# Attention and expert kernel on one core: the loads and weight splits of the first batch, the place of the second expert's split, and the order of row loads, stores and output sums are changed

## The chip, the cores and the metric

The kernel runs on one core of one Trainium2 chip. The metric is the device time of the whole kernel in microseconds (us), the median of three runs. "PE" is TensorE, "DVE" VectorE, "ACT" ScalarE, "POOL" GpSimd, and "SP" the engine that here only issues transfers.

## The reference

Two residual blocks over 16 batches of 128 tokens with 512 features, all in float32:

```python
x = x + tanh(g_xattn) * xattn(layernorm(x), ctx, pos, pos, Wq, Wkv, Wout, bout)
x = x + tanh(g_ffn) * ffn(layernorm(x), gate_w, w1, w2, shared_w1, shared_w2)
# xattn: 32 heads of 16, rotary embedding by position on q and k, softmax over 128 context rows
# ffn:   softmax router over 16 experts, top 6 of them per token; expert: silu(x w1a) * (x w1b) @ w2,
#        width 352; a shared expert of width 704 for every token
```

## The kernel before

Every float32 product is made of three fp32r matmuls. Both factors are split into a "hi" part (a copy rounded to fp32r) and a "lo" part (the value minus hi), and hi·hi, hi·lo and lo·hi are summed in PSUM. So each activation and each weight has a copy (hi) and a subtraction (lo) before PE can use it.

**Phase A** (`phase_a`) is attention, normalisation and routing. It is a software pipeline of rounds. A round works on five batches at once, one for each stage LOAD, PROJECT, ATTEND, TAIL and PLACE, and is cut into eight units `u`. The order of the work in a round is written out by hand for each engine (`one_round`). The first six and the last four rounds are peeled, and what happens once only hangs on them:

- `sync` issues the loads. At the start it issues x of batch 0, Wq, the constants, positions, gates, bout and gate_w, which all count into one semaphore, `small_in`; then the first context, Wkv, Wout and x of batch 1. POOL's first `rsqrt`, PE, ACT and DVE all wait for `small_in`.
- `first_work` on ACT and DVE splits Wq ("q", 128x2048), Wkv ("kv") and Wout ("o"): ACT writes hi, DVE lo. DVE also works out the rotary angles (`first_angles`, seven small instructions), of which ACT takes the sine.
- POOL makes the rotary pairs (`pairs`, two instructions for q and two for k), the inverse deviations (`rsqrt`), and scatters each batch's rows to the experts' lists in DRAM (`scatter`, six indirect transfers). It also splits the experts' weights: `split_w1` (8 copies and 8 subtractions of 128x352) and `split_w2`. The splits of the first expert (place 0) stand in rounds 1 to 3 (`early_weights`), the w1 split of the second one (place 1) in the last round with an ATTEND stage.

**Phase B** (`phase_b`) runs tiles of 128 rows: 6 early tiles of the shared expert, 111 routed blocks, then the rest of the shared expert. Step i of PE is `down(i-2)`, `transpose_act(i-1)`, `up(i)`. Beside it DVE turns the rows of tile i+1 (`turn_x`) and makes `x_low`, `a_low` and `gated` (the activation, whose PE transposition opens the next step); ACT makes `x_high`, `a_high`, `gate` (silu) and copies y out of PSUM (`y_out_of_psum`). SP loads the rows of tile i+3 (`load`: a table value, four transfers for `xr`, one for `xw`), stores y of tile i-2 (`store`), and for the early tiles loads x1 of batch i (`load_x1_early`), to which DVE's `add_early` adds the early tile's result. `add_early` waits for x1 and for the store that last read its y buffer. In the last part `combine_rows` and `combine` sum the six gathered expert rows of each token, and `finish` adds the shared expert's sum in PSUM (`y_banks`) and so sets the bank free.

An order on each engine is fixed when the program is written: an instruction that waits holds up all that stand behind it on its engine.

## Time and profile before

| | |
|---|---|
| Median of three runs | 1397.35 us (1395.98 to 1401.92) |
| Profiled execution, its own time | 1397.16 us |
| Its span, first to last instruction | 1395.0 us |
| PE busy | 1321.3 us, 95% |
| DVE, POOL, ACT busy | 774.5, 697.9, 570.1 us |
| Phase A | about 0 to 480 us |
| Phase B | about 480 us to the end |

The 2.2 us between the span and the profiled execution's own time lie before the first and after the last instruction. The profile shows, per instruction, the start, the duration, and in brackets how long the engine had been idle and what it waited for.

### The profile page before, as it was taken

Reading aid. Unit: us, or ns where it says so; the run is one execution under the profiler, and the core shown is the slowest. Engines: PE = TensorE matmul, PEld = TensorE weight load, DVE = VectorE, ACT = ScalarE, POOL = GpSimd, SP = SyncE. Lnnn points to the kernel's source line nnn. Section 1 sums busy time; section 2 is a strip of 40 time slices with the busy share of each in tenths; the row PEclk is TensorE's granted clock in tenths of the full one; section 3 lists DMA queues with packets and bytes.
Section 4 is the critical chain, followed back from the end, with each engine's and each line's share of the span. In section 5 each row is a group of like instructions: output and inputs, shape, how many; then the busy total and the mean of one; then the engine's idle time right before and its main releaser. Section 6 shows DMA issues by size and latency. Waiting matters only on the chain.

```text
span 1395.0 us, 32586 instructions
## 1 busy us (share of the span) xinstructions
PE 1321.3 (95%) x8414; PEld 1133.8 (81%) x8415; DVE 774.5 (56%) x1572; ACT 570.1 (41%) x1374; POOL 697.9 (50%) x968
## 2 busy tenths in 40 slices
PE   3799999999996898999999999999999999999998
PEld 2566766766764788999999999999999999998887
DVE  4467777777767763444444444444444444356776
ACT  3667667667664422332323333232333323221121
POOL 4354554544545654297442445555542350285673
PEclk9899999999997999999999999999999999999999
DMA  5032332322323665544354444444434443266885
GB/s 202 17 110 83 128 115 80 137 104 80 144 80 108 216 210 182 183 144 133 102 149 146 146 148 144 151 144 141 128 112 148 145 151 85 87 191 206 263 247 157
DMA packets 152398, 196.97 MB, mean 141 GB/s; under 512 B 33155, under 2 KB 103300, under 8 KB 149524
## 3 DMA queue, kind: packets, MB, share of 16 engines
q1 hardware_dynamic: 130292, 104.03, 24.8%
q0 software_dynamic: 22048, 92.23, 19.6%
q8 instruction: 29, 0.48, 0.2%
q14 instruction: 29, 0.24, 0.1%
HBM read 122.11 MB, written 74.07 MB: 141 GB/s over the span
## 4 chain that ended last, share of the span: by engine, by line
PE 75%; DVE 8%; ACT 6%; issue 5%; SPq 2%; DMA 1%; ACTq 0%; DVEq 0%; POOL 0%; POOLq 0%
PE bank L1562 35%; PE bank L1607 19%; PE bank L713 5%; ACT soft L599 4%; PE bank L738 4%; PE bank L1574 3%; PE bank L720 2%; PE bank L752 2%; PE bank L825 2%; DVE smax L1013 2%; PE bank L769 1%; DVE x L1058 1%; DVE attn L1052 1%; DVE stats L1061 1%; SPq L1346 1%
## 5 line engine op out<-in xcount | busy, mean ns | idle before, releaser
L1562 PE MATMUL bank<-w_hi,x_hi 128*128 (+1 forms) x1144 | 289.9, 334 | 0.0
L1562 PE MATMUL bank<-w_hi,x_lo 128*128 (+1 forms) x1144 | 277.1, 323 | 0.0
L1562 PE MATMUL bank<-w_lo,x_hi 128*128 (+1 forms) x1144 | 277.0, 323 | 0.0
L212 POOL CAST w_hi<-w_raw 128x352 fp32r<-128x352 f32 x152 | 72.7, 526 | 369.4 <-PE bank L1562 369.4
L1502 ACT ACTIVATE silu<-bank 128x352 f32<-128x352 f32 x143 | 66.4, 464 | 410.3 <-PE bank L1562 410.3
L1678 DVE SCALAR_TENSOR_TENSOR act<-silu,row_w,bank 128x352 f32<-128x352 f32 x111 | 64.4, 580 | 290.7 <-ACT silu L1502 290.6
L1562 PEld LDWEIGHTS bank<-w_lo,x_hi 128*128 128x128 f32 x1144 | 199.2, 189 | 0.0
L1562 PEld LDWEIGHTS bank<-w_hi,x_lo 128*128 128x128 f32 x1144 | 199.0, 188 | 0.0
L1562 PEld LDWEIGHTS bank<-w_hi,x_hi 128*128 128x128 f32 x1144 | 192.6, 189 | 0.4 <-issue 0.4
L1607 PE MATMUL bank<-w_hi,a_hi 128*128 (+3 forms) x429 | 170.5, 397 | 8.9 <-ACT y L1486 3.8
L599 ACT ACTIVATE soft<-bank,smax 128x128 f32<-128x128 f32 x512 | 146.9, 380 | 76.7 <-DVE smax L1013 76.6
L1607 PE MATMUL bank<-w_lo,a_hi 128*128 (+3 forms) x429 | 170.4, 397 | 0.0
L1607 PE MATMUL bank<-w_hi,a_lo 128*128 (+3 forms) x429 | 169.7, 396 | 0.0
L1491 ACT ACTIVATE x_hi<-x_t 128x512 fp32r<-128x512 f32 x133 | 84.1, 632 | 178.3 <-DVE x_t L1652 178.3
L216 POOL TENSOR_TENSOR w_lo<-w_raw,w_hi 128x352 fp32r<-128x352 f32 x152 | 146.0, 991 | 0.0
L1657 DVE TENSOR_TENSOR x_lo<-x_t,x_hi 128x512 fp32r<-128x512 f32 x133 | 127.4, 958 | 31.1 <-ACT x_hi L1491 26.0
L1433 POOL DMA_INDIRECT gath<-y_rows,y_slots x96 | 101.5, 1057 | 48.0 <-issue 26.5
L1661 DVE TENSOR_TENSOR a_lo<-bank,a_hi 128x384 fp32r<-128x384 f32 x143 | 79.3, 554 | 72.9 <-ACT a_hi L1496 72.0
L520 POOL DMA_INDIRECT expert_rows<-row,slots x96 | 95.6, 996 | 35.5 <-issue 31.7
L1013 DVE TENSOR_REDUCE smax<-bank 128x4 f32<-128x512 f32 x128 | 85.0, 684 | 38.2 <-PE bank L738 37.2
L1607 PEld LDWEIGHTS bank<-w_hi,a_hi 128*128 128x128 f32 (+1 forms) x429 | 81.1, 189 | 22.6 <-issue 7.9
L1652 DVE STREAM_TRANSPOSE x_t<-xr 128x512 f32<-128x512 f32 x133 | 93.7, 704 | 7.9 <-DMA xr<-expert_rows 7.8
(186 smaller groups left out, 2155.4 us busy)
## 6 DMA issues: line engine op xcount, KB each, us to landing
xr<-expert_rows SPq DMA_DIRECT2D x444, 64.0 KB, 1.9
y_rows<-y SPq DMA_DIRECT2D x111, 256.0 KB, 2.1
w_raw<-in_w POOLq DMA_DIRECT2D x19, 1408.0 KB, 6.6
w_raw<-in_w POOLq DMA_DIRECT2D x19, 512.0 KB, 7.8
xr<-x_rows SPq DMA_DIRECT2D x88, 64.0 KB, 3.0
x_t<-x_rows SPq DMA_DIRECT2D x22, 256.0 KB, 4.6
x_sb<-in_x SPq DMA_DIRECT2D x16, 256.0 KB, 3.8
x_res<-in_x SPq DMA_DIRECT2D x16, 256.0 KB, 3.0
```

What stands on the lines that cost most here:

```text
L212: nc.gpsimd.tensor_copy(w1_hi[d][half][:, s], w1_raw[:, d, halves[half]]).then_inc(w_hi_made, 1)
L216: nc.gpsimd.tensor_tensor(w1_lo[d][half][:, s], w1_raw[:, d, halves[half]], w1_hi[d][half][:, s].bitcast(F32), ALU.subtract).then_inc(w1_m ...
L520: g.indirect_dma_start(rows, bass.IndirectOffsetOnAxis(slots[j][:, k:k + 1], 0), row[j][:], None)\
L599: last = a.activation(soft[u % 2][:, h, :], bank[2 + u % 2][:, h * P:(h + 1) * P], ACT.Exp, bias=smax[u % 2][:, h:h + 1])
L1013: v.tensor_reduce(smax[u % 2][:], s3, AX.X, ALU.max, negate=True).then_inc(smax_done, 1)
L1433: nc.gpsimd.indirect_dma_start(gath[b % 2][:, k, :], None, y_rows, bass.IndirectOffsetOnAxis(y_slots[:, b * 8 + k:b * 8 + k + 1], 0))\
L1491: a.activation(x_hi[j][:], x_t[:], ACT.Copy).then_inc(x_hi_done, 1)
L1562: last = nc.tensor.matmul(to[:, 0:WIDTH], xx[jt][:, d, :], w[d][half][:, cols], start=(d == 0 and xx is x_hi and w is w1_hi), stop=(d == D ...
L1607: last = nc.tensor.matmul(to[:], l[j][0:m, c, :], w[c][0:m, cols], start=(first and c == 0 and k == 0), stop=(final and c == 2 and k == 2))
L1652: v.transpose(x_t[:].rearrange("p c (i t) -> p i c t", i=4), xr[j][:].rearrange("p (i c e) -> p i c e", i=4, c=DC)).then_inc(x_turned, 1)
L1657: v.tensor_tensor(x_lo[j][:], x_t[:], x_hi[j][:].bitcast(F32), ALU.subtract).then_inc(x_lo_done, 1)
L1661: v.tensor_tensor(a_lo[j][:].rearrange("p c n -> p (c n)"), a_bank[:, 0:3 * P], a_hi[j][:].rearrange("p c n -> p (c n)").bitcast(F32), ALU ...
```

## The change

**First batch.** The constants are put in a new order, so that those needed first (identity, even/odd scales, frequencies) make a block of 141 columns with a semaphore of its own, `first_in`. The small transfers move from SP's queue to ACT's (gates: to POOL's), with their own semaphores for positions and gates. Wq is split in two parts ("q0", "q1"), Wkv in its k and v columns ("k", "v"). The angles are made before DVE's first `xn`, the "o" split one round earlier, right after the first rotary pairs. ACT runs one small Exp at the end of its first work.

**Second expert.** `split_w1(pool, 1)` is done in two halves at the end of rounds 4 and 5 instead of in one piece in the last ATTEND round.

**Phase B.** SP issues the row loads ahead of the stores, and in step 3 the load of tile 7 as well as that of tile 6. In the steps after the third ACT copies y out of PSUM ahead of `x_high` and DVE does `add_early` ahead of `turn_x`. In the last part `finish` comes ahead of `combine_rows`.

```diff
@@ gpsimd, early_weights and one_round
                 if r == 0:
-                    pool.wait_ge(w_hi_done, 1)
+                    pool.wait_ge(w_hi_done, 3)
                     load_w(nc.gpsimd, 0)
...
+                if r == 4:
+                    split_w1(pool, 1, range(0, 2))
+                if r == 5:
+                    split_w1(pool, 1, range(2, 4))
...
                 if last_round(at, ATTEND):
                     pool.wait_ge(v_mm, BATCHES)
                     clear_act()
-                    split_w1(pool, 1)
@@ scalar
-            act.wait_ge(small_in, 16 * 5)
+            a.dma_start(const[:, 0:C_FIRST], cf[:, 0:C_FIRST]).then_inc(first_in, 16)
+            a.dma_start(pos_in[:], pos).then_inc(pos_sem, 16)
+            a.dma_start(const[:, C_FIRST:C_N], cf[:, C_FIRST:C_N]).then_inc(small_in, 16)
+            a.dma_start(gate_raw[:], gate_w).then_inc(small_in, 16)
+            a.dma_start(bout_b[:], bout).then_inc(small_in, 16)
+            act.wait_ge(gates_in, 16)
             a.activation(tanh2[:], gate2[:], ACT.Tanh).then_inc(tanh_done, 1)
+            act.wait_ge(first_in, 16)
...
                 if u == 1:
                     split_weights("o")
+                    act.wait_ge(small_in, 16 * 3)
                     a.activation(gate_hi, gate_raw[:], ACT.Copy).then_inc(w_hi_done, 1)
+
+                    act.wait_ge(tanh_done, 1)
+                    a.activation(gexp[:, 0:2], tanh2[:], ACT.Exp)
@@ phase_b, sync, one_step
+                if i is None or starts_tile(i, 1):
+                    t, j, n = tile(i, at, 1)
+                    if not isinstance(t, int):
+                        load(*at(3))
+                    elif t + 2 < TILES and i != 4:
+                        load(t + 2, j, n + 1)
+                if i == 3:
+                    load(7, 1, 3)
                 if live(i, -2) and (routed(i, -2) or early(i, -2)):
                     store(*at(-2))
                     if early(i, -2) and early(i, 0):
                         load_x1_early(i)
-                if i is None or starts_tile(i, 1):
-                    t, j, n = tile(i, at, 1)
-                    if not isinstance(t, int):
-                        load(*at(3))
-                    elif t + 2 < TILES:
-                        load(t + 2, j, n + 1)
@@ phase_b, scalar and vector, one_step
                     if halves_first(i):
                         a_high(*at(-1))
+                        if routed(i, -2):
+                            y_out_of_psum(*at(-2))
                     x_high(t, j, n, before)
...
                 if halves_first(i):
                     a_low(*at(-1))
+                    if early(i, -2):
+                        add_early(*at(-2))
...
-                if early(i, -2) and i != 3:
-                    add_early(*at(-2))
                 if shared and i - 1 in sum_at and sum_at[i - 1] < BATCHES - 1:
                     combine(sum_at[i - 1])
+                if shared and i in finish_at:
+                    finish(finish_at[i])
                 if shared and i in sum_at:
                     combine_rows(sum_at[i])
-                if shared and i in finish_at:
-                    finish(finish_at[i])
```

**Order on DVE, start of the program.** The names are those of the tiles: `soft` holds the angles, `w_lo` the lo parts of Wq and Wkv. Before:

```order
L981 BN_AGGR mean<-stats 128x2 [waits stats1_done]
L986 TENSOR_SCALAR xn<-x_sb,mean,rstd 128x512 [waits rstd1_done,var1]
L924 TENSOR_TENSOR soft<-pos_in,const 128x16x4 [waits small_in]
...
L937 SCALAR_TENSOR_TENSOR soft<-soft 128x256 [waits angles]
L943 TENSOR_TENSOR w_lo<-w_raw,w_hi 128x2048 [waits w_hi_done]
L993 TENSOR_TENSOR xt_lo<-bank,xt_hi 128x512 [waits xt_hi_done,tanh_done,init_done]
L943 TENSOR_TENSOR w_lo<-w_raw,w_hi 128x2048 [waits w_hi_done]
L998 TENSOR_TENSOR c_lo<-c_raw,c_hi 128x256 [waits c_hi_done,sincos_done]
```

The same place on DVE now:

```order
L1011 BN_AGGR mean<-stats 128x2 [waits stats1_done]
L949 TENSOR_TENSOR soft<-pos_in,const 128x16x4 [waits pos_in_sem,first_in]
...
L962 SCALAR_TENSOR_TENSOR soft<-soft 128x256 [waits angles]
L1016 TENSOR_SCALAR xn<-x_sb,mean,rstd 128x512 [waits rstd1_done,var1]
L968 TENSOR_TENSOR w_lo<-w_raw,w_hi 128x1024 [waits w_hi_done]
L1023 TENSOR_TENSOR xt_lo<-bank,xt_hi 128x512 [waits xt_hi_done,tanh_done,init_done]
L968 TENSOR_TENSOR w_lo<-w_raw,w_hi 128x1024 [waits w_hi_done]
L968 TENSOR_TENSOR w_lo<-w_raw,w_hi 128x2x512 [waits w_hi_done]
```

The seven angle instructions moved ahead of `xn`, and only half of Wq's lo part now stands ahead of `xt_lo`.

**Order on SP, where phase B's own steps begin (step 3).** `x_rows<-y` is a store of an early tile, `x_t<-x_rows` the load of x1, `xr<-expert_rows` a row load, and the wait for `table_in` is the wait for the routing table. Before:

```order
L468 DMA table<-block_table 1x444 [waits table_out]
L1364 DMA x_rows<-y 128x512 [waits scattered0,scattered1,table_in,pads_out0,x2_out1,y_done,x2_out0,x1_out]
L1368 DMA x_t<-x_rows 128x512 [waits y_done]
L1341 TENSOR_LOAD table
...
L1346 DMA xr<-expert_rows 32x4x128
L1359 ISA
L1359 DMA xw<-expert_rows 128x16
L1337 TENSOR_LOAD pad_at [waits pad_zero]
```

The same place on SP now:

```order
L469 DMA table<-block_table 1x444 [waits table_out]
L1371 TENSOR_LOAD table [waits scattered0,table_in,scattered1,x2_out1,pads_out0,x2_out0,x1_out]
...
L1389 DMA xw<-expert_rows 128x16
L1371 TENSOR_LOAD table
...
L1389 DMA xw<-expert_rows 128x16
L1394 DMA x_rows<-y 128x512 [waits y_done]
L1398 DMA x_t<-x_rows 128x512 [waits y_done]
L1367 TENSOR_LOAD pad_at [waits pad_zero]
```

Two whole row loads (tiles 6 and 7) now stand ahead of the store of tile 1 and the load of x1 for batch 3.

## Rows read from the trace of the kernel before

**Rows 1.** Busy time by engine in one stretch, with granted clock (PEclk)
```profile
420.00:450.00 30.00, 18.45 (x138) 12.62 (x140) 22.61 (x39) 14.38 (x41) 18.83 (x30) 0.72 0.37 125
```

**Rows 2.** Timeline, first batch: start us, us, engine line, operation, [idle before <-releaser]
```profile
1.16 0.42 SPq L409 DMA_DIRECT2D w_raw<-in_wq  x1
...
8.79 0.19 POOL L497 TENSOR_SCALAR neg_half<-mean 128x1 f32<-128x1 f32 x1 [5.99 <-DMA gate_raw<-in_gate_w]
...
11.04 0.55 DVE L986 TENSOR_SCALAR xn<-x_sb,mean,rstd 128x512 f32<-128x512 f32 x1 [6.89 <-POOL rstd L508]
...
13.83 2.29 DVE L943 TENSOR_TENSOR w_lo<-w_raw,w_hi 128x2048 fp32r<-128x2048 f32 x1
...
16.86 0.77 PE L713 MATMUL bank<-w_hi,xt_hi 128*128 128x512 f32 x1 [4.04 <-DVE xt_lo L993]
...
30.21 0.79 PE L713 MATMUL bank<-w_hi,c_hi 128*128 128x512 f32 x1 [1.36 <-ACT k_t L659]
```

**Rows 3.** DMA issues, first 9 us: KB each, median us to landing
```profile
w_raw<-in_wq SPq DMA_DIRECT2D x1, 1024.0 KB, 5.4
```

**Rows 4.** Timeline, second and third round
```profile
35.82 1.28 ACT L599 ACT_TABLE_LOAD   x1
...
48.75 2.28 DVE L943 TENSOR_TENSOR wo_lo<-wo_raw,wo_hi 128x2048 fp32r<-128x2048 f32 x1
...
53.63 1.41 PE L738 MATMUL bank<-k_t,q_t 32*128 32x256 f32 x8 [4.03 <-ACT soft L599]
```

**Rows 5.** Timeline, POOL's half split in round 1, and the start of a full round
```profile
29.81 1.94 POOL L212 CAST w_hi<-w_raw 128x352 fp32r<-128x352 f32 x4
...
31.72 3.59 POOL L216 TENSOR_TENSOR w_lo<-w_raw,w_hi 128x352 fp32r<-128x352 f32 x4
...
122.09 0.84 POOL L488 TENSOR_TENSOR q_cos<-q_cos,q_sin 128x256 f32<-128x256 f32 x1 [1.14 <-DVE q_sin L972]
...
127.03 0.66 PE L720 MATMUL bank<-const,q_cos 128*128 128x128 f32 x4
```

**Rows 6.** Timeline, the last round with an ATTEND stage
```profile
433.31 10.26 DVE L1657 TENSOR_TENSOR x_lo<-x_t,x_hi 128x512 fp32r<-128x512 f32 x1
...
435.93 7.09 POOL L216 TENSOR_TENSOR w_lo<-w_raw,w_hi 128x352 fp32r<-128x352 f32 x8
...
444.32 1.11 PE L720 MATMUL bank<-const,attn 128*128 128x128 f32 x4 [9.75 <-DVE attn L1037]
```

**Rows 7.** Line L1657, whole run: duration ns min/median/max
```profile
L1657 DVE TENSOR_TENSOR x_lo<-x_t,x_hi x133: 677/693/10260, 433.3 to 1369.2; 128x512 fp32r<-128x512 f32 x133
```

**Rows 8.** Timeline, first steps of phase B
```profile
503.00 0.42 SPq L1368 DMA_DIRECT2D x_t<-x_rows  x1
...
506.65 0.35 SPq L1359 DMA_DIRECT2D xw<-expert_rows  x1
...
508.06 0.71 DVE L1652 STREAM_TRANSPOSE x_t<-xr 128x512 f32<-128x512 f32 x1 [1.90 <-DMA xr<-expert_rows]
...
510.33 0.68 DVE L1707 TENSOR_TENSOR y<-bank,x_t 128x512 f32<-128x512 f32 x1
...
511.56 0.55 PE L1574 MATMUL bank<-const,act 128*128 128x128 f32 x3 [0.58 <-DVE act L1678]
...
539.69 0.79 PE L1607 MATMUL bank<-w_hi,a_hi 128*128 x1 [3.85 <-ACT y L1486]
```

**Rows 9.** Line L1368 (loads of x1), 500 to 516 us
```profile
DMA to landing us min/median/max: 2.7/2.8/2.9
```

**Rows 10.** The chain that ended last: start us, us, what
```profile
539.69 4.20 PE bank L1607 x9
...
549.05 2.09 PE bank L1607 x9
```

**Rows 11.** Timeline, shared expert's last part
```profile
1262.82 1.76 DVE L1685 TENSOR_TENSOR tree<-gath 128x1536 f32<-128x1536 f32 x1
...
1265.33 0.47 PE L1607 MATMUL bank<-w_hi,a_hi 128*128 128x512 f32 x1 [2.40 <-DVE o_t L1701]
```

More of the change, by code:

```diff
@@ L63 @@
 ROUND = 12582912.0
-C_ID, C_UP, C_ONE = 0, 128, 256
-C_IOTA = 384
+C_ID = 0
+C_EVEN = 128
+C_ODD = C_EVEN + 1
+C_P = C_ODD + 1
+C_DUMP = C_P + 1
+C_HALF = C_DUMP + 1
+C_FREQ = C_HALF + 1
+C_FIRST = C_FREQ + 8
+C_UP, C_ONE = C_FIRST, C_FIRST + 128
+C_IOTA = C_ONE + 128
 C_CAP = C_IOTA + 16
@@ L349, in phase_a @@
         slots = two("slots", [P, 8], U32)
-        small_in = sem("small_in")
-        w_in = {name: sem(f"w_in_{name}") for name in parts}
+        small_in, first_in, pos_sem, gates_in = sem("small_in"), sem("first_in"), sem("pos_in_sem"), sem("gates_in")
+        w_in = {name: sem(f"w_in_{name}") for name in ("q", "kv", "o")}
+        q_part = [[w.rearrange("p (c n) -> p c n", c=DC)[:, 2 * k:2 * k + 2] for w in parts["q"]] for k in range(2)]
+        kv_part = [[w.rearrange("p (c n) -> p c n", c=CC)[:, :, D * k:D * (k + 1)] for w in parts["kv"]] for k in range(2)]
+        split = {"q0": ("q", q_part[0]), "q1": ("q", q_part[1]), "k": ("kv", kv_part[0]), "v": ("kv", kv_part[1]),
+                 "o": ("o", parts["o"])}
         w_hi_done, w_lo_done = sem("w_hi_done"), sem("w_lo_done")
@@ L574, in scalar @@
             a = nc.scalar
-            act.wait_ge(small_in, 16 * 5)
+            a.dma_start(const[:, 0:C_FIRST], cf[:, 0:C_FIRST]).then_inc(first_in, 16)
[4 more added lines that the diff above has]
+            act.wait_ge(gates_in, 16)
             a.activation(tanh2[:], gate2[:], ACT.Tanh).then_inc(tanh_done, 1)
+            act.wait_ge(first_in, 16)
             def split_weights(name):
-                raw, hi, lo = parts[name]
-                act.wait_ge(w_in[name], 16)
+                whole_name, (raw, hi, lo) = split[name]
+                act.wait_ge(w_in[whole_name], 16)
                 a.activation(hi, raw, ACT.Copy).then_inc(w_hi_done, 1)
@@ L781, in project @@
                     pe.wait_ge(xt_lo_done, b + 1)
-                    three(bank[0][:], xt, q_w, DC, lambda t, c: t[:, c, :], lambda w, c: w[:, c, :]).then_inc(q_mm, 1)
+                    three(bank[0][:], xt, q_w, DC, lambda t, c: t[:, c, :], lambda w, c: w[:, c, :],
+                          (lambda: pe.wait_ge(w_lo_done, 2)) if isinstance(b, int) and b == 0 else (lambda: None))\
+                        .then_inc(q_mm, 1)
                 if u == 2:
                     if isinstance(b, int) and b == 0:
-                        pe.wait_ge(w_lo_done, 2)
+                        pe.wait_ge(w_lo_done, 3)
+                        pe.wait_ge(small_in, 16 * 3)
                     pe.wait_ge(c_lo_done, b + 1)
@@ L800, in project_late @@
                 if u == 7:
+                    if isinstance(b, int) and b == 0:
+                        pe.wait_ge(w_lo_done, 4)
                     pe.wait_ge(kt_done, 2 * (b + 1))
@@ L919, in first_angles @@
             def first_angles():
-                dve.wait_ge(small_in, 16 * 5)
+                dve.wait_ge(first_in, 16)
+                dve.wait_ge(pos_sem, 16)
                 for p in range(2):
@@ L940, in split_weights @@
             def split_weights(n, name):
-                raw, hi, lo = parts[name]
+                raw, hi, lo = split[name][1]
                 dve.wait_ge(w_hi_done, n + 1)
@@ L947, in first_work @@
                 if at(LOAD) and at(LOAD)[0] == 0:
+                    if u == 2:
+                        first_angles()
                     if u == 7:
-                        first_angles()
-                        split_weights(0, "q")
+                        split_weights(0, "q0")
                         dve.wait_ge(init_done, 4)
@@ L954, in first_work @@
                     if u == 0:
-                        split_weights(1, "kv")
+                        split_weights(1, "q1")
+                        split_weights(2, "k")
                         dve.wait_ge(sincos_done, 1)
+                    if u == 1:
+                        split_weights(3, "v")
                     if u == 2:
@@ L959, in first_work @@
                             v.memset(bank[6 + k][:], 0.0).then_inc(psum_zeros, 1)
-                if at(PROJECT) and at(PROJECT)[0] == 1:
-                    if u == 2:
-                        split_weights(2, "o")
-                        dve.wait_ge(w_hi_done, 4)
+                    if u == 3:
+                        dve.wait_ge(k_rope_done, 1)
+                        split_weights(4, "o")
+                        dve.wait_ge(small_in, 16 * 3)
+                        dve.wait_ge(w_hi_done, 6)
                         v.tensor_tensor(gate_lo, gate_raw[:], gate_hi.bitcast(F32), ALU.subtract)\
@@ L1513, in one_step @@
                         a_high(*at(-1))
+                        if routed(i, -2):
+                            y_out_of_psum(*at(-2))
                     x_high(t, j, n, before)
-                if live(i, -2) and routed(i, -2):
+                if live(i, -2) and routed(i, -2) and not halves_first(i):
                     y_out_of_psum(*at(-2))
```

32 lines of the change are left out of this document (13 added, 19 removed).

## The prediction

> **What bounds the kernel now.** PE is busy 95% of the span, and in the routed part of phase B it is busy without a gap, so nothing that the change does to SP, ACT or DVE there can shorten it. What can be won lies where PE stands still or runs at the lower granted clock. I read the windows first: they show such stretches at the start, at 420 to 450 us (PE busy 18.45 of 30 us, granted clock 0.72 [rows 1]), in the first steps of phase B, and in the last part. Then I read the timeline of each, for what ended last before PE started again, and the chain for what follows a gap. PE stands at 1.2 GHz for a while after one: the nine matmuls of `down` at 539.69 take 4.20 us, right after 3.85 us of idling, and 2.09 us at 549.05 [rows 8, 10]. So a gap costs its length and then some: here 2.1 us for the nine and, as I estimate from them, 1 us for what follows until the clock is back.
>
> **The start, 5.4 us won.** POOL's first `rsqrt` starts at 8.79 us, when the last small transfer has landed; `xn` follows at 11.04, and the first Wq matmul at 16.86, since `xt_lo` stands behind the angles and all of Wq's lo part (2.29 us from 13.83) [rows 2]. Now the small block and the positions are first on a queue of their own. Wq is issued at 1.16 us and lands after 5.4 us, at 6.6 [rows 2, 3]. No row shows two queues at the start. I take the positions to land 1 us ahead of Wq, at 5.6: they start with it and are tiny, but share the DMA engines with it. Angles 2.2 us (what lies between the end of `xn` at 11.59 and 13.83), `xn` 0.55, then 2.9 us for transposition, `xt_hi`, half a lo part and `xt_lo` (an estimate: the 5.3 us from 11.59 to 16.86 less the angles' 2.2, less 0.2 for the shorter split) give a first matmul at 11.3, 5.5 us earlier. All that follows up to the v projection at 30.21 moves with it; there DVE has one more small split in its way, so I take 5.4. Bounds: 4.0 if positions land 1.5 us later than that, well behind Wq; 6.9 if they are early, when Wq's own 6.6 and two half copies hold `xt_hi`. First expert's weights: their load waits for two more copies, 3 us, but its split stands at 29.81 [rows 5], long after.
>
> The Trainium skill ("DMA: Bandwidth & Descriptors", Issuing engines are not separate DMA queues) says that transfers from different engines run on the same 16 DMA engines and interleave, so that spreading them saves issue time only. By that alone the small ones would land hardly earlier. It speaks for the low bound; what no row shows is the interleaving itself.
>
> **Second and third round, 5.0 us won.** ACT's load of the Exp table (1.28 us at 35.82 [rows 4]) stands ahead of the first softmax; it is now done at the start behind the "o" copy, where ACT waits for PE. I take 1.2. The "o" lo part (2.28 us at 48.75) and the gate's stand ahead of a row maximum; the softmax behind it ends 4.03 us of PE idling at 53.63 [rows 4]. Moved to where DVE waits for k's pairs, they free 3.1 us, of which 2.2 count, since the copy of q is next in ACT's way. PE then stays at its clock: of the 4 us after 53.63 I give back 1.6 (between nothing and the 3.1 of above). If the cover fails (DVE's idle time in the first batch), the 2.28 us come back there, and POOL's `rsqrt` waits with it.
>
> **The second expert's split, 11.3 won, 3.4 lost.** In the last ATTEND round `x_lo` takes 10.26 us, against a median of 0.693 [rows 6, 7]. It begins during POOL's copies and ends when POOL's eight subtractions, 7.09 us from 435.93, end; then PE transposes attn at 444.32 after 9.75 us of idling [rows 6]. Without the split beside it `x_lo` ends at 434.0, and PE starts 9.4 us earlier. What is late next is only the ordinary chain of the round. And PE keeps its clock; for the 6 us after 444.32 I take 1.9, two thirds of the price above, since half of that time is waiting for ACT and DVE anyway. Bounds: 9.4 and 12.5.
>
> The work now stands in rounds 4 and 5 behind the scatters. A half takes 1.94 + 3.59 = 5.5 us [rows 5]. POOL's next work, the q pairs, starts at 122.09 after only 1.14 us of idling, ends 1.8 us later, at 123.9, and PE wants it at 127.03 [rows 5]. So the pairs come 5.5 - 1.14 = 4.4 us (with issue, 4.8) later, at 128.7, 1.7 us after PE wants them; behind this PE transposition wait ACT's copy of q and its softmax. The k pairs and the next `rsqrt` fit behind. Twice 1.7 is 3.4. Bounds: nothing, and 2 x 5.5 = 11.
>
> **Phase B, first steps: nothing.** Two things lie against each other. Won: the row load of tile 10 is late, since SP is a step behind; y and the next `down` wait behind it, 3.85 us of PE, and 3.1 at the low clock [rows 8, 10]; with another 0.8 where `add_early` held the y bank, 7.8. With two loads at once SP no longer lags. Lost: SP holds the x1 load of batch 3 at 503.00 and then a row load until 507.0 [rows 8], 3.6 us a row load. Now two of these stand ahead of the store of tile 1 and of that x1 load, which is issued at 502.5 + 7.2 + 0.4 = 510.1 (502.5: half a us ahead of the 503.00, where the wait for the table ended and the store was issued) and lands 2.8 us later [rows 9], at 512.9. `add_early` of tile 3 waits for both, and it now stands ahead of `turn_x`. So `turn_x`, before at 508.06 [rows 8], starts at 513.6, and behind it queue `x_high` and silu on ACT, `x_low` and the activation on DVE, 3.5 us from 508.06 to 511.56, when PE transposes [rows 8]. That becomes 516.7 or so: 5.1 us of PE, and 3 at the low clock, 8.1. I put the difference of 0.3 at zero. Bounds: 8 won, 3 lost.
>
> **Last part, 3.2 us won.** PE waits 2.40 us for `finish`, which stood behind `combine_rows` (1.76 us) [rows 11]. Now it comes first: 1.76, and most of the low clock after it (1.4, from the 2.1 of above for a shorter gap). Elsewhere `gated` waits for both in any order. Copies of y ahead of `x_high` cost nothing: tiles are turned a step ahead.
>
> **Sum.** 5.4 + 5.0 + 11.3 - 3.4 + 0 + 3.2 = 21.5. From the profiled execution's 1397.16 us (span 1395.0, as good as the median of 1397.35): **1375.7 us**.
>
> **Rivals.**
> - *Phase B wins in full.* If the x1 load is no hindrance, 7.8 more are won: 1367.9. For it: the lost side is the longer chain of estimates, and every us that SP or the table comes earlier against PE shrinks it. Against: between 503.00 and 507.0 SP's rows leave no gap that could be saved, and x1 is late by more than 2 us.
> - *The blocked read moves along.* `x_lo` was held for all of POOL's run. If a DVE instruction with such a fate falls into each half, 5.5 us and a lower clock for each, 10 us in all, instead of 3.4: near 1383. Against: `c_lo` and the others that read two SBUF tiles seem to lie outside these 5.5 us. The Trainium skill ("SBUF — State Buffer", Who interferes with whom) says that a DVE instruction with two SBUF inputs and a GpSimd one that reads SBUF lock each other out for one whole instruction. That would be 1 us, not 9.6; the trace disagrees, and by the rule this rival would be worth 2 us at most.
> - *Small transfers are hardly faster.* If they share the DMA engines evenly with Wq and land behind it, 1.5 us later than I take, the start wins 4.0 and the time is 1377.1; if they come as late as all of them do now (8.79 [rows 2]), it wins only what the half splits give, about 1: 1380. The page named above would have it so.
> - *Slower.* In the routed loop the store now stands behind a row load, 3.6 us later. ACT copies y into the same buffer two steps on, with some 5 us to spare as I estimate (12.5 us, less the copy, the load and 2.8 for landing). If the store came over 5 us later, PE would wait in each of 111 blocks; 0.3 us of it makes +33, less 21.5: 1409. It decides only from there.
>
> **How the numbers follow.** A measurement of this kernel tells 0.5%, 7 us, from no change. Chances: my sum (1371 to 1380) 50%; phase B in full 20%; blocked read 12%; transfers 10%; slower 3%; the rest on both sides. The range that takes in the first four and leaves under 2 in 10: 1365 to 1388. Faster by over 0.5% (below 1390.4) 93%, within 4%, slower 3%.
>
> **What would show it.** Right: first Wq matmul near 11.3 us; no Exp table load at the first softmax; no `x_lo` above 2 us, and attn transposed some 0.9 us after it; q transposed 1 to 2 us late in rounds 5 and 6; DVE waiting for x1 or the store at `add_early` of tile 3, and PE idle about 5 us there; no late row load ahead of tile 10; `finish` without PE waiting. Wrong: a long DVE instruction beside a half split, or PE gaps in the routed loop.

## The result, and the profile after

| | median, us | executions | range, us |
|---|---|---|---|
| before, first timing | 1396.89 | 4 | 1395.98 to 1401.92 |
| after, first timing | 1380.83 | 4 | 1375.91 to 1385.33 |
| before, second timing | 1397.33 | 11 | 1396.10 to 1401.16 |
| after, second timing (e10) | 1378.62 | 4 | 1376.50 to 1381.51 |

The change makes the kernel faster: the ratio of the times is 0.9877 with a 95% interval of 0.9835 to 0.9919, and 0.9861 (0.9843 to 0.9880) in the second timing; 16 to 19 us. The profiled execution of after took 1375.91 us (span 1374.1 us), 21.25 us less than that of before. It is the fastest of the eight that were timed, so the sum of the prediction, 21.5 us, has to be held against two traces and, apart from that, against the medians.

The timeline of after, at the places that answer to [rows 2], [rows 4], [rows 5], [rows 6] and [rows 8] (start us, us, engine and line, operation, and in brackets the idle time before it and what ended it):

```profile
0.71 0.41 ACTq L580 DMA_DIRECT2D const<-in_cf  x1
1.16 0.45 ACTq L581 DMA_DIRECT2D pos_in<-in_pos  x1
...
4.97 0.19 POOL L499 TENSOR_SCALAR neg_half<-mean 128x1 f32<-128x1 f32 x1 [0.92 <-DVE mean L1011]
...
7.07 0.36 DVE L949 TENSOR_TENSOR soft<-pos_in,const 128x64 f32<-128x64 f32 x2 [2.20 <-DMA pos_in<-in_pos]
...
9.19 0.54 DVE L1016 TENSOR_SCALAR xn<-x_sb,mean,rstd 128x512 f32<-128x512 f32 x1
...
12.57 0.77 PE L732 MATMUL bank<-w_hi,xt_hi 128*128 128x512 f32 x1 [1.60 <-DVE xt_lo L1023]
...
26.16 0.77 PE L732 MATMUL bank<-w_hi,c_hi 128*128 128x512 f32 x1 [1.45 <-ACT k_t L675]
...
113.46 3.61 POOL L218 TENSOR_TENSOR w_lo<-w_raw,w_hi 128x352 fp32r<-128x352 f32 x4
117.04 0.84 POOL L490 TENSOR_TENSOR q_cos<-q_cos,q_sin 128x256 f32<-128x256 f32 x1
...
118.85 0.66 PE L739 MATMUL bank<-const,q_cos 128*128 128x128 f32 x4 [0.95 <-POOL q_cos L492]
...
426.03 0.68 DVE L1691 TENSOR_TENSOR x_lo<-x_t,x_hi 128x512 fp32r<-128x512 f32 x1
...
428.21 1.09 PE L739 MATMUL bank<-const,attn 128*128 128x128 f32 x4 [0.81 <-ACT gexp L697]
...
491.08 0.35 SPq L1389 DMA_DIRECT2D xw<-expert_rows  x1
491.48 0.43 SPq L1394 DMA_DIRECT2D x_rows<-y  x1
491.95 0.43 SPq L1398 DMA_DIRECT2D x_t<-x_rows  x1
...
494.80 0.69 DVE L1741 TENSOR_TENSOR y<-bank,x_t 128x512 f32<-128x512 f32 x1 [6.58 <-DMA x_t<-x_rows]
...
498.23 0.90 PE L1608 MATMUL bank<-const,act 128*128 128x128 f32 x3 [5.19 <-DVE act L1712]
```

The first `rsqrt` starts at 4.97 us where it stood at 8.79, and the first Wq matmul at 12.57 where it stood at 16.86 [rows 2]; between them DVE waits for the positions, not for the small block. The half split's subtractions begin at 113.46 and POOL's pairs follow them at 117.04 without idling: PE waits 0.95 us for the pairs. `x_lo` takes 0.68 us where it took 10.26 [rows 6]. And at 494.80 the wait stands that the prediction put there: y of tile 3 waits for x1, and PE 5.19 us for the activation queued behind it.

Two more views of after, busy time with granted clock (PE, PEld, DVE, ACT, POOL, then PEclk), and what PE waited for from 1150 to 1380 us (total, times, longest):

```profile
420.00:450.00 30.00, 26.32 (x205) 18.82 (x204) 18.38 (x53) 17.77 (x52) 12.49 (x19) 0.83 0.60 196
...
500.00:505.00 5.00, 5.00 (x21) 5.00 (x20) 2.20 (x5) 0.63 (x1) 2.06 (x3) 0.57 0.64 196
```

```profile
PE bank L1608 <- DVE act L1712: 4.3, 5, 1.3
PE bank L1641 <- DVE a_lo L1695: 1.8, 1, 1.8
PE bank L1641 <- DVE o_t L1735: 0.7, 1, 0.7
```

PE is busy 26.3 us of the stretch in which it was busy 18.45 [rows 1]. When PE starts again at 498.23 after its gap, it runs at 1.2 GHz up to 504.3 us (the granted clock is 0.57 of full speed from 500 to 505). `finish` costs PE 0.7 us instead of 2.4 [rows 11].

### The profile page after: what moved, and what is told of

It reads as the page before. It is cut to its first block, busy times and chain, and to the rows that moved or that the text cites. A ratio compares the mean times of both kernels' runs of the same rounds, so it can differ in the third digit from the quotient of the medians.

```text
span 1374.1 us, 32642 instructions
## 1 busy us (share of the span) xinstructions
PE 1316.0 (96%) x8414; PEld 1131.0 (82%) x8415; DVE 764.6 (56%) x1574; ACT 571.5 (42%) x1377; POOL 697.7 (51%) x969
## 4 chain that ended last, share of the span: by engine, by line
PE 75%; DVE 10%; ACT 6%; issue 4%; POOL 2%; DMA 2%; SPq 1%; ACTq 0%; DVEq 0%; POOLq 0%
PE bank L1596 36%; PE bank L1641 19%; PE bank L732 5%; ACT soft L615 4%; PE bank L757 4%; PE bank L1608 3%; PE bank L739 2%; PE bank L849 2%; DVE smax L1043 2%; PE bank L771 2%; DMA x_t<-x_rows 1%; PE bank L788 1%; DVE tree L1719 1%; POOL expert_rows L522 1%; DVE x L1088 1%
## 5 line engine op out<-in xcount | busy, mean ns | idle before, releaser
L1691 DVE TENSOR_TENSOR x_lo<-x_t,x_hi 128x512 fp32r<-128x512 f32 x133 | 118.7, 892 | 34.1 <-ACT x_hi L1523 28.8
L1641 PEld LDWEIGHTS bank<-w_hi,a_lo 128*128 128x128 f32 (+1 forms) x429 | 80.6, 188 | 18.2
```

The costliest lines, as they stand in the source:

```text
L1641: last = nc.tensor.matmul(to[:], l[j][0:m, c, :], w[c][0:m, cols], start=(first and c == 0 and k == 0), stop=(final and c == 2 and k == 2))
L1691: v.tensor_tensor(x_lo[j][:], x_t[:], x_hi[j][:].bitcast(F32), ALU.subtract).then_inc(x_lo_done, 1)
```

## How the traces are compared

Single times of one kernel lie up to 14 us apart (e4), so each trace is cut at the same events of the program, and the lengths of the stretches are compared. The events are DVE's cast of the slots of batch 1, 3 and 13 (the last steps of phase A's rounds), and the 5th, 14th, 121st, 126th and last activation of phase B. Worked out from the timelines, in us; "split at" says where the second expert's w1 is split.

```
kernel            split at       to 1st  rounds  rounds  last A.  first   routed  shared  shared
                                 slots   to 3rd  to 13th to B     steps   loop    finish  rest
before            last ATTEND    112.74   51.76  258.98   79.70   65.20  670.04   35.51  112.48
e1_split_only     rounds 4, 5    112.51   53.41  258.94   71.10   63.51  674.14   33.93  112.14
e2_start_only     last ATTEND    105.52   51.81  259.11   76.50   63.34  670.09   35.36  112.16
e3_order_only     last ATTEND    115.93   51.76  258.97   76.41   65.06  672.07   32.27  112.04
e5_pool_apart     same, gaps     115.81   51.83  259.18   68.40   63.31  672.54   35.49  112.15
e6_clear_last     last ATTEND    112.80   51.83  259.14   78.96   63.34  670.64   33.93  112.17
e7_dve_pause      last ATTEND    112.79   51.83  259.12   80.36   61.79  670.11   33.93  112.19
e9_one_gap        same, one gap  114.22   51.81  259.03   69.94   63.20  674.22   33.95  112.16
after             rounds 4, 5    103.52   53.41  259.25   69.04   64.51  670.06   32.29  113.37
e10_after_again   rounds 4, 5    104.79   53.40  258.97   70.81   63.41  672.06   32.28  112.44
e4_x1_first       rounds 4, 5    103.68   53.42  258.92   69.66   57.06  670.06   32.28  112.63
e8_gap            rsqrt, 4, 5    108.19   52.34  259.12   70.43   62.05  670.06   32.28  112.05
e11_x1_gap        rsqrt, 4, 5    105.52   52.31  258.99   68.97   62.28  670.05   32.28  112.45
e12_apart_b       rsqrt, 4, 5    104.18   52.36  259.26   69.76   57.92  670.06   32.27  113.21
```

The seven traces with the old start take from 112.5 to 115.9 us up to the first slots, with the same code. It goes with the clock: in e3 the granted clock is 0.57 of full speed from 50 to 60 us and in before 0.83, though their first Wq matmuls are only 0.1 us apart. Added up from the granted clock of each trace, PE stood at 1.2 GHz in this first stretch for 17.1 us in the four traces at 112.5 to 112.8, for 20.5 us in e9 (114.2) and for 27.3 us in e3 and e5 (115.9 and 115.8). With the new start it was 10.2 us in after, e4 and e12 (103.5 to 104.2) and 13.7 us in e2, e10 and e11 (104.8 to 105.5). The column "shared finish" divides in the same way: with `finish` behind `combine_rows` it is 33.9 in the traces in which PE kept full speed there, and 35.4 or 35.5 in those with 3.4 us at 1.2 GHz. The routed loop has steps of 2 us, of which more below.

## The experiments

**e1, the split alone.** Only this is changed in the kernel before:

```diff
                     load_after_split(pool, 1)
+                if r == 4:
+                    split_w1(pool, 1, range(0, 2))
+                if r == 5:
+                    split_w1(pool, 1, range(2, 4))
...
                 if last_round(at, ATTEND):
                     pool.wait_ge(v_mm, BATCHES)
                     clear_act()
-                    split_w1(pool, 1)
```

> The kernel before with one part of the change: the second expert's w1 split in two halves in rounds 4 and 5, none in the last ATTEND round. Theory (x_lo was held by the split beside it): x_lo of that round takes 0.7 us instead of 10.26, which gives 9.3 us, and 1 to 2 us of low clock; the halves cost 0.8 to 1.0 us each, as the trace of after shows at the first one. Net 8 to 9 us: a profiled time of 1388 to 1389 us against 1397.2. Rival (what held x_lo is not the split but the place: the copies of ACT, the row loads of SP beside it): x_lo still takes several us, and the time is 1397 to 1399.

Measured: 1390.26 us (10 executions) against 1398.87 (22 of before), ratio 0.9944 (0.9923 to 0.9965); profiled 1390.42. `x_lo` took 0.68 us. The halves cost 1.65 us (column "rounds to 3rd"), the last ATTEND round is 8.6 us shorter, as the theory has it. But the routed loop is 4.1 us longer, by two events of 2 us, at 767 and 995 us. The timeline of e1 at the first of them:

```profile
757.37 7.29 POOL L216 TENSOR_TENSOR w_lo<-w_raw,w_hi 128x352 fp32r<-128x352 f32 x8
...
762.01 4.86 DVE L1660 TENSOR_TENSOR x_lo<-x_t,x_hi 128x512 fp32r<-128x512 f32 x1
...
764.61 1.72 POOL L224 CAST w_hi<-w_raw 128x512 fp32r<-128x512 f32 x3
...
766.41 4.58 POOL L227 TENSOR_TENSOR w_lo<-w_raw,w_hi 128x512 fp32r<-128x512 f32 x3
...
767.47 0.49 PE L1610 MATMUL bank<-w_hi,a_hi 128*128 x1 [1.63 <-DVE a_lo L1664]
```

This is the held read again, in the middle of the routed loop: `x_lo` begins while POOL subtracts and takes 4.86 us. It ends 0.54 us behind 766.33, where POOL waits for its last copy and has its first gap (0.08 us). PE waits 1.63 us for `a_lo`, which is next on DVE. So the hold is no speciality of the round in which the kernel before shows it.

**e2, the start alone**: all hunks of the diff that touch the first batches.

> The kernel before with the parts of the change that touch the first batches alone (queues, weight splits in parts, Exp table, o split); the second expert's split stays whole in the last ATTEND round. Theory: the first scatter group of round 4 ends 9.2 us earlier, as in after, and all of it stays: 1388 us. Rival: part of it is lost again in rounds 5 to 16 (the trace of after is 7.3 us ahead at the last ATTEND round where it was 9.2 ahead at 112 us, and the halves account for 1.6): 1389 to 1390 and less than 9 us ahead at the last ATTEND round. On the held read: if x_lo is held whenever it meets POOL's run there, it takes about 10 us again; if the phase of one moment decided it, it may take 1 to 2 us, and the time is then 1378 to 1380.

Measured: 1390.21 us (7 executions), ratio 0.9928 (0.9901 to 0.9956); profiled 1384.37. `x_lo` took 9.31 us. The start won 7.2 us and none of it was lost up to the last ATTEND round. The theory's 9.2 was one execution's: six traces with the new start (all but e8, whose queue differs) reach the first slots at 103.5 to 105.5, on average 104.5, seven with the old one on average 113.8. The start wins 9.3 us on average. The profiled execution is 3.6 us faster than expected, mostly in the last ATTEND round, which is 3.2 us shorter than in before although `x_lo` was held.

**e3, the order in phase B alone**: SP's, ACT's and DVE's hunks of phase B.

> The kernel before with the parts of the change that touch phase B alone (row loads ahead of stores, copies of y ahead of x_high, add_early ahead of turn_x, finish ahead of combine_rows). Theory, from the prediction: the first steps of phase B come out even (7.8 us won, 8.1 lost), the last part wins 3.2: 1394 us, with y of tile 3 waiting for x1 and PE idle about 5 us there. Rival: finish wins only its own 1.7 us, since PE's clock is back at once: 1395.5. x_lo of the last ATTEND round takes about 10 us, as before, if its hold is a rule of that place; if it was the chance of one execution, 1 to 2 us.

Measured: 1396.97 us (10 executions), ratio 0.9984 (0.9965 to 1.0003), which is not told from no change; profiled 1395.26. The first steps come out even (65.06 against 65.20), with y of tile 3 waiting 6.93 us for x1 and PE 6.09. The shared part is 3.24 us shorter. `x_lo` was held 9.28 us, and once more in the loop (4.77 us at 689.11), which took back 2 us. By the medians of this timing e1, e2 and e3 win 8.6, 8.7 and 1.9 us, 19.2 in all, near the 16.1 and 18.7 us of the whole change.

**e4, x1 first.** The changed kernel with one edit in SP's step 3:

```diff
                 if i == EARLY - 3:
+                    store(*at(-2))
+                    load_x1_early(i)
                     rows_complete()
...
-                if live(i, -2) and (routed(i, -2) or early(i, -2)):
+                if i != EARLY - 3 and live(i, -2) and (routed(i, -2) or early(i, -2)):
```

> The changed kernel with one thing more: SP's step 3 issues the store of tile 1 and the x1 load of tile 3 ahead of the wait for the table and of the two row loads. Theory: y of tile 3 no longer waits 6.6 us for x1 and PE no longer 5.2 us for the activation behind it; with the low clock behind the gap (18 matmuls of up at 0.59 us instead of 0.32 each for most of them, 2.6 us) 7.8 us are won: 1368 us profiled against 1375.9. Rival: the row load of tile 6, now next to last of the two, lands no later, but turn_x of that tile starts earlier and waits for it instead: PE still stands still for 2 to 3 us, and the time is 1371 to 1373. Second rival: the wait only moves one step on, to the x1 load of tile 4 or the row load of tile 8, and nothing is won: 1376.

Measured: 1375.42 us (4 executions), ratio to before 0.9846 (0.9798 to 0.9894); profiled 1369.58 (span 1367.7). The timeline of e4:

```profile
483.85 1.38 SPq L1398 DMA_DIRECT2D x_t<-x_rows  x1
...
488.61 0.68 DVE L1743 TENSOR_TENSOR y<-bank,x_t 128x512 f32<-128x512 f32 x1
```

x1 is issued at 483.85, while SP waited for the table anyway, and y of tile 3 starts with no idle time before it. The first steps take 57.06 us instead of 64.51 and 63.41: 6.9 us on average, near the 7.8 expected. The wait was SP's order. PE also kept full speed through these steps, where it stood at 1.2 GHz for 6.8 us in after. This is shown by the traces alone: e4's median is 5.4 and 3.2 us below the two timings of the changed kernel, but with 4 executions each, whose ranges overlap, that is not told from no change.

**e5, e6, e7 and e9, what holds `x_lo`.** All are the kernel before with one edit in the last ATTEND round:

```diff
 e5: a wait behind each of POOL's instructions in this split
+                    if apart:
+                        pool.wait_ge(w_hi_made, 11 * e + 2 * d + half + 1)
...
+                    if apart:
+                        pool.wait_ge(w1_made, 8 * e + 2 * d + half + 1)
 e6: split_w1(pool, 1) ahead of clear_act() instead of behind it
 e7: DVE, u == 2
+                            dve.wait_ge(smax_done, (BATCHES - 1) * GROUPS + u + 1)
                             x_low(0, 0, 0)
 e9: one wait between copies and subtractions
+            if gap:
+                pool.wait_ge(w_hi_made, 11 * e + 8)
```

> The kernel before, where in the last ATTEND round POOL waits for each of its own copies and subtractions to end before it issues the next, so that its run has a small gap behind every instruction. Theory (POOL's unbroken run keeps x_lo out): with gaps x_lo gets its turn behind one or two POOL instructions and takes 1 to 2 us; PE transposes attn 7 to 9 us earlier than in the kernel before, and the profiled time is near 1389. Rival (something else in that place holds x_lo until the split is over, whether POOL pauses or not): x_lo takes about 10 us or more, and ends 0.6 us behind POOL's last subtraction, as in the three executions that show it so far. Sixty-odd x_lo of phase B that met such a run of POOL took 1.7 us at most, which speaks for some condition beside the unbroken run; this run tells whether a gap is enough.

> The kernel before, with the two memsets of act (POOL, 0.8 us) behind the second expert's split in the last ATTEND round instead of ahead of it. The split follows the scatters at once and starts 0.7 us earlier against x_lo. Theory A (the place of x_lo against the run, or what comes right ahead of it on POOL, makes the difference to phase B, where no memset and no scatter stands ahead): x_lo takes 1 to 2 us. Theory B (the memsets have no part in it): x_lo is held to the end of the run again, 9 to 10 us, and also past the memsets only if these count as part of the run.

> The kernel before, where DVE in the last ATTEND round waits for its own row maximum to end before it issues x_lo of tile 0 (x_lo then starts 0.1 to 0.2 us later, into an empty DVE). In phase B x_lo mostly starts after a wait of 0.4 to 0.7 us for ACT; here it starts right behind another DVE instruction. Theory A (back-to-back issue on DVE makes it lose the port): x_lo takes 1 to 2 us, and the profiled time is near 1389. Theory B (DVE's side has no part in it): about 9 to 10 us again, the time as before.

> The kernel before with one wait more: in the last ATTEND round POOL waits, between its eight copies and its eight subtractions, for the last copy to end. Theory (x_lo is kept out until the first gap in POOL's run, as the w2 split's own wait ended a hold of 4.86 us in phase B of the kernel with the split alone): x_lo starts during the copies and ends 0.6 to 0.7 us behind them, after 2 to 3.5 us in all, with the subtractions starting a little later; PE starts 6 to 7 us earlier there and the profiled time is 1390 to 1391. Rival (one short gap is not enough, it takes several, or the hold lasts to the end of the run): 9 to 10 us, 1397. If x_lo happens to start behind the copies, neither is told apart.

Measured, one execution each: 1390.85, 1393.54, 1394.46 and 1390.72 us; before took 1395.95 us in its one execution beside the first three and 1397.33 in the median of 11 beside e9. Single times lie too far apart to be read closely, so `x_lo` itself is looked at. The timelines of e5, e6, e7 and e9, in this order:

```profile
435.87 4.64 POOL L212 CAST w_hi<-w_raw 128x352 fp32r<-128x352 f32 x8
...
436.68 0.77 DVE L1661 TENSOR_TENSOR x_lo<-x_t,x_hi 128x512 fp32r<-128x512 f32 x1
```

```profile
433.77 9.41 DVE L1657 TENSOR_TENSOR x_lo<-x_t,x_hi 128x512 fp32r<-128x512 f32 x1
```

```profile
433.85 10.01 DVE L1658 TENSOR_TENSOR x_lo<-x_t,x_hi 128x512 fp32r<-128x512 f32 x1
```

```profile
434.10 3.89 POOL L212 CAST w_hi<-w_raw 128x352 fp32r<-128x352 f32 x8
...
435.84 1.82 DVE L1659 TENSOR_TENSOR x_lo<-x_t,x_hi 128x512 fp32r<-128x512 f32 x1
```

With a gap behind every POOL instruction `x_lo` gets through at once beside the copies, which take 4.64 instead of 3.44 us. Neither the memsets (e6) nor the issue right behind another DVE instruction (e7) are needed for it: held again. In e6 `x_lo` ends at 443.18 while the two memsets still run (to 443.34), so it did not wait for them. e9 tells less than it was made for: `x_lo` ended at 437.66, 0.33 us before the copies did and so before the added gap. It was let in between two copies, with no gap there, and neither theory said so. So one execution of e5 does not prove either that the gaps let it in.

**e8, the halves in POOL's idle time, positions first.** Added to e4: the halves stand behind the `rsqrt` of rounds 4 and 5, and ACT's queue issues the positions ahead of the small block.

```diff
                     rsqrt(mean1, rstd1, newton1, rstd1_done, b)
+                    if isinstance(b, int) and b in (4, 5):
+                        split_w1(pool, 1, range(2 * b - 8, 2 * b - 6))
```

> The kernel of the run x1_first with two things more: the half splits of rounds 4 and 5 stand behind POOL's rsqrt for the next batch instead of behind the scatters, where POOL is idle for 5 us even in the rounds with a half (so 9 to 10 us without one), and the positions are first on ACT's queue, ahead of the small block. Theory: a half of 5.4 us fits into that idle time and costs nothing, so the 0.95 and 0.70 us that the kernel with the split alone lost are won back; angles run beside rsqrt and xn starts 1.5 to 2 us earlier than 9.37. Together 3 to 4 us: 1364 us profiled, if PE's clock comes back at the same places. Rival: DVE's subtractions with two SBUF inputs meet the halves there (c_lo), PE waits for one, and the cost is 1 to 5 us instead; and with x and the positions on two queues at once x itself lands later, so that xn gains under 1 us: 1367 to 1371.

Measured, one execution: 1376.97 us, slower than e4's fastest. The halves did what was hoped, 0.5 us lost instead of 1.65 (52.34 against an average of 51.80 without any). The queue did the opposite. DMA issues of e8, the first 4 us (KB each, us to landing), the small block being the one of 70.5 KB:

```profile
const<-in_cf ACTq DMA_DIRECT2D x1, 70.5 KB, 6.6
...
pos_in<-in_pos ACTq DMA_DIRECT2D x1, 16.0 KB, 3.0
```

In after the small block is first and lands after 3.4 us, the positions second after 5.8. In e8 it is 3.0 for the positions and 6.6 for the block, and `rsqrt` starts at 7.98 instead of 4.97; the first slots come at 108.19, where the other traces with the new start average 104.5. In both traces the transfer that stands ahead of Wq (issued at 1.16) is through quickly, and the one issued with it lands with it. As that one is also the second on its queue, these two causes are not told apart. e8 also has a PE wait of 2.71 us at 524.85 that e4 has not.

**e10, e11, e12, timed together.** e10 is the changed kernel. e11 is e4 with the halves behind `rsqrt` and the start as in the changed kernel. e12 is e11 with e5's waits in all splits of phase B, for w1 and w2.

> The changed kernel as it is, timed again beside the next two. It is expected at a median of 1379 to 1382 with executions from 1375 to 1386. The spread of it and of all others is, by the traces so far, where PE's clock comes back in the first 62 us (up to 3.3 us apart between two executions of the same first batches) and whether one or two x_lo of phase B are held (1.9 us each).

> The changed kernel with the x1 load of tile 3 ahead of the row loads and the half splits of rounds 4 and 5 in POOL's idle time behind rsqrt, the queues at the start as in the changed kernel. From the traces: x1 first wins 7.0, the halves in the idle time 1.1 (0.58 lost instead of 1.66). Theory: 8 us below the changed kernel, 1372 to 1373 in the median. Rival (the gap in the first steps of phase B only changes its place, as the kernel gap had 2.7 us of PE waiting for y at 524.9 where x1_first had none): 4 to 6 us below.

> The kernel of x1_gap, where POOL waits behind every instruction of the splits in phase B for its end (the splits take a third longer, 14 instead of 10.5 us for w1, in some 20 us of idle time). Theory: no x_lo of phase B can be held for more than one POOL instruction; four such holds of 4.8 us were in ten traces, at 1.9 us of PE each, so the median falls by 0.5 to 1 us and the slowest executions by 2 to 4. Rival (the longer splits come late for PE where experts are short, or in the last expert's split ahead of the gathers): 2 us or more slower than x1_gap.

Measured: 1378.62 (4 executions), 1377.60 (6, from 1373.31 to 1385.91) and 1371.23 us (5, from 1369.45 to 1376.58). The ratios to before (1397.33) are 0.9861, 0.9872 (0.9846 to 0.9897) and 0.9819 (0.9801 to 0.9838). e12 is the fastest version, 26 us below before and, by medians, 7.4 below the changed kernel.

e11 won hardly anything, and its trace shows the rival that its expectation named. Timeline of e11, and under it the landing of the store at 510.67 (its line, 509 to 512 us):

```profile
509.81 0.61 POOL L203 DMA_DIRECT2D w_raw<-in_w  x1 [0.59 <-POOL w_lo L229]
...
510.67 0.42 SPq L1392 DMA_DIRECT2D x_rows<-y  x1
...
519.84 0.60 ACT L1518 ACTIVATE y<-bank 128x512 f32<-128x512 f32 x1 [5.00 <-DMA x_rows<-y]
...
520.67 0.49 PE L1641 MATMUL bank<-w_hi,a_hi 128*128 x1 [2.51 <-ACT y L1518]
```

```profile
DMA to landing us min/median/max: 9.1/9.1/9.1
```

POOL issues an expert's weights, 2.1 MB, from 509.81 on. The store of y is issued 0.9 us later and takes 9.1 us, against 2.1 in the median of all stores of y. ACT's copy into the same buffer waits for it, with `x_high` behind, and PE stands still. In e4 the store goes out at 509.37, only 0.06 us behind the weights at 509.31, and takes 2.4 us: PE does not wait for y; in e12, whose longer splits put the weights at 512.11, the store at 510.04 is 2 us ahead. The column "first steps" shows it: 57.1 and 57.9 us where the store is not held up, 62.1 and 62.3 where it is (in e8 it took 8.7 us, issued 1.3 us behind the weights). So 4.4 us between the traces of e11 and e12, which differ by 3.9 in all, are this and not the held read, which e11's trace does not have. It is a side effect of the longer splits, and not what e12 was expected to win by. What made the other executions of e11 slower is not known: the trace is of its fastest. In e12 no `x_lo` takes over 1.46 us, but 53 that began beside a split of phase B are too few to tell: 7 of 643 were held in the other thirteen traces.

## Why the prediction was right, and where it was not

**The start (5.4): 4.3 at the first Wq matmul, 4.05 at the v projection.** This is the low bound, and for the reason it named. I took the positions to land at 5.6 us; they landed at 7.0, after 5.8 us, just after Wq (ACT begins to copy it at 6.84), and in e8 the block that stood in their place did the same. The rest of the estimate held: 5.5 us from the angles to the first matmul, where 5.65 were taken. The positions' issue (start us, us) and landing (KB, us from issue) in before, then their landing in after:

```profile
2.10 0.43 SPq L411 DMA_DIRECT2D pos_in<-in_pos  x1
pos_in<-in_pos SPq DMA_DIRECT2D x1, 16.0 KB, 5.1
...
pos_in<-in_pos ACTq DMA_DIRECT2D x1, 16.0 KB, 5.8
```

So the positions landed at 7.2 before and at 7.0 after. What won the 4.3 us is not an earlier landing of them: the angles no longer wait for the last small transfer (8.8), `rsqrt` and `xn` are no longer ahead of them, and half a lo part stands behind them instead of a whole one. The Trainium skill ("DMA: Bandwidth & Descriptors", Issuing engines are not separate DMA queues) says that transfers started by different engines run on the same DMA engines and interleave, so that spreading them saves only issue time. The trace agrees for the positions. It disagrees for the small block, which I had taken to land hardly earlier as well: issued 0.45 us ahead of Wq, it landed at 4.1, where the constants as one load had landed at 7.0.

**Second and third round (5.0): 5.2.** From 4.05 at the v projection to 9.2 us at the first slots. The Exp table is loaded at 17.49 us, where ACT waits for PE, and `wo_lo` stands at 23.57, beside a POOL `neg_half` that takes 2.29 us instead of 0.19, so that `rsqrt` waited with it. No run separated the terms of this step. PE stood at 1.2 GHz for 10.2 us up to the first slots and for 17.1 in before. The average of the start as a whole is 9.3 against 10.4 predicted.

**The halves (-3.4): -1.65.** The right place and wait, half the size. The working had POOL's pairs 4.8 us later and PE waiting 1.7 us for them. The half took 5.3 us with no issue time behind it, which put the pairs 4.2 us later (117.04, against 122.09 less the 9.2 won before), and PE waited 0.95 and 0.70 us.

**The last ATTEND round (11.3): 10.7 in the two traces, 8.6 on average.** From the 13th slots to the fifth activation of phase B the five traces with a held `x_lo` take 78.4 us and the nine with a free one 69.8. The held time itself is 8.6 to 9.6 us; of the 1.9 for the clock 1.1 came on top in the two traces, and nothing on average. One cause shows in after: PE then waits 0.81 us for ACT (`gexp`), where the estimate had only the ordinary chain.

**Phase B, first steps (0, as 7.8 won and 8.1 lost): 8.3 won, 7.6 lost.** Counted by activations, after is 17.97 us ahead at the 5th, 10.37 at the 8th, and 18.65 at the 12th. e3 shows the same alone, e4 that the loss is SP's order. The near balance is in part luck. The lost side was mis-added: 513.6 plus 3.5 is 517.1 and not 516.7, so 5.5 us of PE and 8.5 in all, with a net loss of 0.7 where 0.7 was won. PE waited 5.19 us, since the chain behind y of tile 3 took 3.43 us (494.80 to 498.23) where these terms have 4.2. And one step of the reasoning was incomplete though the size was right: I said that the row load of tile 10 was late because SP was a step behind. Two views of before, the timeline and the windows, show the rest of the cause:

```profile
527.13 0.61 POOL L201 DMA_DIRECT2D w_raw<-in_w  x1 [0.58 <-POOL w_lo L227]
...
537.59 0.71 DVE L1652 STREAM_TRANSPOSE x_t<-xr 128x512 f32<-128x512 f32 x1 [4.48 <-DMA xr<-expert_rows]
```

```profile
530.00:535.00 5.00, 5.00 (x31) 4.66 (x30) 1.14 (x2) 0.58 (x2) 0.00 (x0) 1.00 0.94 325
```

The rows were issued from 526.87 to 528.8, beside an expert's weights, the DMA engines were 0.94 busy, and the rows took over 8 us. A step earlier they go ahead of the weights (in after at 510.40, the weights at 514.20). It is the mechanism that cost e11's traced execution its gain.

**The last part (3.2): 3.22 in the two traces, 2.3 on average.** PE waits 0.7 instead of 2.4 us [rows 11]. Without the edit the stretch takes 33.9, 35.4 or 35.5 us, with it 32.3 each time. e1 (33.93) and e2 (35.36) both wait 2.4 us for `finish`; in e1 the clock stays at full speed and in e2 it falls for 3.4 us. So the wait itself is worth 1.65 us, and the other 1.5, the prediction's term for the clock, comes only in some executions (3 of the 7 traces without the edit).

**The sum.** In the two traces 21.25 us against 21.5. Over all traces the parts give 9.3 - 1.65 + 8.6 - 0.9 + 2.3 = 17.7 (the first steps: 64.3 on average with the new order, 63.4 with the old), between the 16.1 and 18.7 of the medians. The prediction worked from one trace with a long hold and a late clock; that size, 3 to 4 us, is what it overstates. That the two traces come within 0.3 us of the sum is luck: the halves cost 1.75 us less than predicted and the first steps won 0.7, against 1.2 too much at the start, 0.6 in the last ATTEND round and 0.9 lost in the last column, which no term covers.

**The rivals.** Phase B in full did not come, since x1 did hinder; e4 made it. The blocked read did not move into the halves: no `x_lo` stands there, and in after no DVE instruction beside the halves took over 0.15 us more than its median. "Slower" did not come in the loop: 670.0 to 670.7 us in all traces without a hold there. Its mechanism, a store behind others that ACT waits for, is real and came in the first steps, by way of the weights. The hardly faster transfers came for the positions alone.

**The held read.** Shown: it needs the split beside it (e1), it does not need the memsets or a DVE instruction right ahead, and with gaps in POOL's run it was not seen. The Trainium skill ("SBUF — State Buffer", Who interferes with whom) says that the two lock each other out for one whole instruction. Of the 643 that began beside a split in phase B 636 agree: at most 1.87 us. The 7 others, near 4.8 us, and 5 of 5 in the last ATTEND round of kernels with an unbroken run there, do not. All 12 end in the same way, 0.55 us behind the last copy or subtraction before the first gap in POOL's run, or before its end. So the hold lasts to the first gap; what decides whether it begins is open. A moment within POOL's instruction seems to matter: 5 of the 7 began 0.112 to 0.117 us into a subtraction of w1, where 7 began in all. But e9 was let in beside copies that do not differ from those of before. An experiment that shifts `x_lo` in small steps was not made.

## What to carry to other kernels

Look at the longest single instruction of a line beside its median: here one of 133 told of 9 us, and in the routed loop the same event comes and goes at 2 us. Before a transfer is put ahead of another, look at which ones are waited for and at what large load is issued near them: a transfer of 256 KB that takes 2.1 us in the median took 9.1 issued 0.9 us behind the first part of 2 MB, and 2.4 issued 0.06 us behind it. The first steps of phase B took 57.1 us in e4 and 62.3 in e11, whose code is the same there, with that store 0.8 us later against the weights. And compare stretches between the same events over several traces before giving a cause to 3 us.

## What the runs showed of the hardware that was not expected

- A DVE subtraction with two SBUF inputs took 9.3 to 10.3 us beside an unbroken run of 16 POOL instructions, of which 12 to 15 passed meanwhile, and 4.8 us in the loop, each time ending 0.55 us behind the run's last before a gap; mostly it took less than 1.9 us under what look like the same conditions.
- The clock's return differs between executions of the same code with the same first events: seven traces of the old start differ by 3.4 us at 112 us (17.1 to 27.3 us of it at 1.2 GHz), six of the new by 2.0 (10.2 to 13.7 us).
- Of two small transfers on one queue, 0.45 us apart, the first took 3.0 to 3.4 us and the second 5.8 to 6.6, whichever was which, with a load of 1 MB issued on another queue at the moment of the second.
